# Cross attention of layer 2: keys projected first, key norms beside the queries, query norms in the score factors

## The chip, the cores and the metric

The kernel runs on one core of a Trainium2 chip. A core has five engines that run side by side and meet only through semaphores: TensorE (PE, matmul, writes the 8 banks of PSUM), VectorE (DVE), ScalarE (ACT), GpSimd (POOL) and SyncE (SP, which issues the loads here). The metric is the device time of one execution in microseconds (us), median of several runs.

## The reference, cut to what matters

x is 8 batches of 64 tokens of width 256 (512 tokens), the context 8 batches of 128 tokens (1024). Six residual stages follow each other: cross attention, attention and mixture of experts of layer 1, then the same three of layer 2. The change lies in the fourth, and touches the end of the third:

```python
def rms_norm(x, scale, eps=EPS):
    ms = jnp.mean(jnp.square(x), axis=-1, keepdims=True)
    return x * jax.lax.rsqrt(ms + eps) * scale
...
img_ctx = context[:, :N_IMG]
q = rms_norm(x @ q_w + q_b, nq_s).reshape(B, S, H, D)
k_img = rms_norm(img_ctx @ ki_w + ki_b, nki_s).reshape(B, -1, H, D)
v_img = (img_ctx @ vi_w + vi_b).reshape(B, -1, H, D)
out_img = sdpa(q, k_img, v_img)
return out @ o_w + o_b
```

The context has 128 tokens, fewer than N_IMG = 257, so all are image context and the text branch is over no tokens; H is 16, D 128. The norm of a query or key is over all 2048 features, that is over all 16 heads, so that no score is final before the last head is projected. x enters through a layernorm; the context doesn't, so the keys need nothing of the stages before.

## The kernel before, in words

Each matmul with weights is made of three (`mm3`, L153 to L155: hi x hi, hi x lo, lo x hi). ACT rounds a weight block to its hi part (`hi_part`, L206), POOL makes the lo part from it (`lo_part`, L215, raw minus hi). Blocks have a part a and a part b, two buffers each; `a_split`, `b_split` count finished parts, `a_used`, `b_used` parts that PE is done with. SP loads the next raw block once the split before it is made (`load_block`, L182 and L185).

The layer 2 cross attention (l1x) starts with the layernorm: DVE normalizes xn (L264), PE transposes it (L295) after `y_start` has put the output bias into banks 6 and 7 (L314), ACT and DVE write xt_hi and xt_lo (L303, L278). All of that waits for x, which the experts stage finishes with `ffn_add_half` (L1127), after its last `down` on PE.

Projections: for each head m, `proj_pe` makes 6 matmuls of 512 columns for the queries (part a, bank 4 + m%2), then 12 for the keys (part b, two banks). `proj_act` squares the queries out of PSUM (L1238) into sq and, one head late, the keys (`proj_keys`, L1228). POOL sums the squares of the queries (L1372), DVE those of the keys (`proj_acc`, L1245), with a wait for its own result behind it; DVE stores queries (qst, L1250, scaled by nqk) and keys (L1255). kst and qst keep all 16 heads.

Norms: when all sums are there, PE sums acc over the partitions (12 products with one column, L1323), DVE makes the variance (L1485), POOL the power -0.5 (L1382), DVE 12 diagonal tiles (L1487), PE spreads them over all partitions (3 banks, L1327), DVE places the key factors in rk (L1492), ACT copies the query factors to rq (L1418).

Attention: for each head ACT copies the keys to kn (L1446) and POOL multiplies the queries with rq into qn (L1389); PE makes the scores from both (`key_scores`, L1266), DVE multiplies them with rk (L1499) and goes through the softmax with ACT; PE transposes the weights (`turn_x`, L1275), mixes the context (`mix_ctx`, L1287), projects values (`values_x`) and output (`out_x`). PE's order is written out in `turn(m, u)`: turn_x(m-2), key_scores(m), values_x(m-3), mix_ctx(m-2), out_x(m-4). First and last turns are written out, the others are in a loop of the sequencer (`Fori`).

## Time and profile before

| | |
|---|---|
| median of 3 runs | 994.69 us (994.02 to 995.31) |
| the profiled execution | 994.79 us |
| its span in the trace | 993.0 us |
| PE busy | 880.0 us (89%) |
| DVE, ACT, POOL busy | 606.5, 427.2, 386.4 us |
| mean granted clock of PE | 0.864 |

A row of the timeline reads: start, duration, engine, line, operation, output<-inputs, how many were merged, and in brackets the idle time before with the one who ended it. PE's clock has two levels, 1.2 and 2.4 GHz; in a stretch 0.50 is all at the lower, 1.00 all at the higher. PEld is the load of weights and lies beside PE. Idle time of an engine that no one waits for costs nothing.

### The profile page before, as it was taken

To read this page: it belongs to the slowest core of one execution; us is meant where nothing else is said; L and a number is where in the kernel's file an instruction comes from. 1 tells how busy PE (TensorE), PEld (TensorE's weight loads), DVE (VectorE), ACT (ScalarE), POOL (GpSimd) and SP (SyncE) were. 2 spreads that over 40 slices of the span, in tenths; PEclk is the share of its full clock that TensorE was granted. 3 is DMA by queue.
4 is the path that set the end of the run, shared out by engine and by line. 5 is a ranking of instruction groups with operands and counts; after the bars stand their busy time and mean duration, and the time that the engine had idled before them with its cause. 6 is when DMAs were issued, how large, how long until landed. Compare 5 with 4: busy or idle time off the path is not lost.

```text
span 993.0 us, 17411 instructions
## 1 busy us (share of the span) xinstructions
PE 880.0 (89%) x6128; PEld 715.5 (72%) x6128; DVE 606.5 (61%) x931; ACT 427.2 (43%) x730; POOL 386.4 (39%) x414
## 2 busy tenths in 40 slices
PE   6489996899999599799769999978898699999997
PEld 5233334789889488588648999857887588888886
DVE  5989984466666457578556666445666344544543
ACT  2268882334433244255325555412222244555452
POOL 2168884133222134378423333111221144444442
PEclk8755555899999589699858999977999699999999
DMA  4059893022111023112100111100110123333331
GB/s 166 0 106 181 161 185 65 22 65 61 45 63 42 27 64 85 43 56 65 39 1 17 33 35 33 42 32 22 43 42 26 32 76 95 91 87 96 89 94 52
DMA packets 102530, 64.00 MB, mean 64 GB/s; under 512 B 71761, under 2 KB 90705, under 8 KB 102354
## 3 DMA queue, kind: packets, MB, share of 16 engines
q1 hardware_dynamic: 102482, 63.37, 24.6%
q8 instruction: 29, 0.48, 0.2%
q14 instruction: 19, 0.16, 0.1%
HBM read 46.05 MB, written 0.52 MB: 47 GB/s over the span
## 4 chain that ended last, share of the span: by engine, by line
PE 71%; DVE 13%; POOL 6%; issue 4%; ACT 3%; DMA 2%; SPq 0%; DVEq 0%; POOLq 0%; ACTq 0%
PE ps L153 18%; PE ps L155 16%; PE ps L154 16%; PE ps L1287 6%; POOL vf L609 4%; PE ps L1565 2%; PE ps L869 2%; PE ps L1566 2%; PE ps L1266 2%; DVE soft L1741 1%; POOL nb L616 1%; PE ps L880 1%; PE ps L314 1%; PE ps L1584 1%; DMA pti<-kres 1%
## 5 line engine op out<-in xcount | busy, mean ns | idle before, releaser
L215 POOL TENSOR_TENSOR wa_lo<-raw,wa_hi 128x512 fp32r<-128x512 f32 (+2 forms) x112 | 147.0, 1313 | 173.1 <-ACT wa_hi L206 170.3
L215 POOL TENSOR_TENSOR wb_lo<-raw,wb_hi 128x256 fp32r<-128x256 f32 (+1 forms) x112 | 92.0, 822 | 289.7 <-ACT wb_hi L206 289.7
L153 PE MATMUL ps<-xt_hi,wa_hi 128*128 128x512 f32 x352 | 147.8, 420 | 6.8 <-DVE xt_lo L278 4.4
L155 PE MATMUL ps<-xt_hi,wa_lo 128*128 128x512 f32 x352 | 144.4, 410 | 0.0
L154 PE MATMUL ps<-xt_lo,wa_hi 128*128 128x512 f32 x352 | 144.2, 410 | 0.0
L677 ACT ACTIVATE kres<-ps,nb,qs 128x1024 int16<-128x1024 f32 x64 | 77.0, 1203 | 28.3 <-POOL nb L616 26.1
L1111 DVE TENSOR_TENSOR hh<-sg,ps 128x512 f32<-128x512 f32 x56 | 38.5, 688 | 79.1 <-PE ps L155 74.4
L153 PEld LDWEIGHTS ps<-xt_hi,wa_hi 128*128 128x128 f32 x352 | 69.5, 198 | 22.7 <-issue 4.8
L798 DVE TENSOR_REDUCE nm<-ps 128x1 f32<-128x1024 f32 x64 | 78.1, 1223 | 10.3 <-PE ps L556 8.9
L1113 DVE TENSOR_TENSOR h_lo<-hh,h_hi 128x512 fp32r<-128x512 f32 x56 | 58.3, 1042 | 40.6 <-ACT h_hi L1103 40.6
L206 ACT ACTIVATE wa_hi<-raw 128x512 fp32r<-128x512 f32 (+2 forms) x112 | 66.7, 595 | 35.7 <-PE ps L155 30.5
L155 PEld LDWEIGHTS ps<-xt_hi,wa_lo 128*128 128x128 f32 x352 | 69.5, 198 | 16.6
L154 PEld LDWEIGHTS ps<-xt_lo,wa_hi 128*128 128x128 f32 x352 | 69.8, 198 | 13.0
L153 PE MATMUL ps<-wb_hi,h_hi 128*128 128x256 f32 (+1 forms) x240 | 68.1, 289 | 4.3 <-DVE h_lo L1113 4.3
L609 POOL CAST vf<-pti 128x1024 bf16<-128x1024 int16 x64 | 66.2, 1036 | 7.0 <-DMA pti<-kres 3.5
L556 PE MATMUL ps<-qkt 48*128 48x512 bf16 x128 | 64.8, 618 | 4.5 <-ACT kres L677 1.5
L1097 ACT ACTIVATE sg<-ps 128x512 f32<-128x512 f32 x56 | 33.5, 598 | 79.7 <-PE ps L155 79.7
L154 PE MATMUL ps<-wb_lo,h_hi 128*128 128x256 f32 (+1 forms) x240 | 66.8, 283 | 0.0
L155 PE MATMUL ps<-wb_hi,h_lo 128*128 128x256 f32 (+1 forms) x240 | 66.8, 283 | 0.0
L1287 PEld LDWEIGHTS ps<-ptx,ctx 128*128 128x128 f32 x512 | 62.8, 201 | 1.9 <-issue 0.6
L153 PE MATMUL ps<-wb_hi,ot_hi 128*128 128x256 f32 x192 | 60.1, 313 | 4.1 <-DVE ot_lo L1717 2.5
L1287 PE MATMUL ps<-ptx,ctx 128*128 128x64 f32 x512 | 62.3, 283 | 0.2 <-ACT ptx L1428 0.2
(254 smaller groups left out, 2016.3 us busy)
## 6 DMA issues: line engine op xcount, KB each, us to landing
raw<-w_l1f SPq DMA_DIRECT2D x44, 256.0 KB, 2.7
raw<-w_l0a SPq DMA_DIRECT2D x16, 384.0 KB, 3.2
raw<-w_l1f SPq DMA_DIRECT2D x44, 128.0 KB, 2.0
raw<-w_l1p SPq DMA_DIRECT2D x32, 128.0 KB, 2.1
raw<-w_l1x SPq DMA_DIRECT2D x32, 128.0 KB, 2.1
raw<-w_l1a SPq DMA_DIRECT2D x16, 256.0 KB, 3.0
raw<-w_l0f SPq DMA_DIRECT2D x12, 256.0 KB, 2.7
raw<-w_l0a SPq DMA_DIRECT2D x16, 128.0 KB, 2.3
```

Source lines behind the costliest of these rows:

```text
L153: nc.tensor.matmul(o, a[0], b[0], start=start, stop=False, **kw)
L154: nc.tensor.matmul(o, a[0], b[1], start=False, stop=False, **kw)
L155: return nc.tensor.matmul(o, a[1], b[0], start=False, stop=stop, **kw)
L206: nc.scalar.activation(dst[:, u, 0:cols.stop - cols.start], raw[:, u, cols], ACT.Copy).then_inc(done, 1)
L215: nc.gpsimd.tensor_tensor(lo[:, u, 0:w], raw[:, u, cols], hi[:, u, 0:w].bitcast(F32), ALU.subtract).then_inc(done, 1)
L556: last = nc.tensor.matmul(slot(n)[:, j * 512:(j + 1) * 512], qkt[64 * a:64 * a + 48, u, t * P:(t + 1) * P], qkt[64 * a:64 * a + 48, u, NTO ...
L609: nc.gpsimd.tensor_copy(pt[:, r, :], pti[:, r, :]).then_inc(x0["pt"], 1)
L677: nc.scalar.activation(ei[:, n % RING, :], slot(n), ACT.Exp, bias=nb[:, n % 3:n % 3 + 1], scale=qs[:, col:col + 1], accum_out=sums[:, u, k ...
L798: nc.vector.tensor_reduce(nm[:, n % 3:n % 3 + 1], slot(n), AX.X, ALU.max, negate=True).then_inc(x0["nm"], 1)
L1111: nc.vector.tensor_tensor(hh[:, u, :], sg[:, u, :], ps[:, 2 * u + 1, :], ALU.mult).then_inc(ff["h"], 1)
L1113: nc.vector.tensor_tensor(h_lo[:, u, :], hh[:, u, :], h_hi[:, u, :].bitcast(F32), ALU.subtract).then_inc(ff["hlo"], 1)
L1287: last = nc.tensor.matmul(ps[:, 3 + c, b * T:(b + 1) * T], ctx[:, b, c * P:(c + 1) * P], ptx[:, g, T * p:T * (p + 1)], start=True, stop=True)
```

## The change

All 16 key projections come first, directly behind the last down projection of the experts stage; y_start and the layernorm's transposes stand on PE behind key 2, the 16 query projections behind key 15. Weights are loaded in that order, as 32 parts of 128 x 256, alternating between the a and the b buffers (`load_projections`). ACT and POOL make three of these parts still in the experts stage or right behind it. Queries have three banks (3, 0, 1), keys two pairs (2, 3 and 4, 5). The squares of the queries are summed in two accumulators: POOL takes heads 1, 5, 7, 9, 11 and 13, DVE the other ten. The key norms are made between the queries: column sums behind query 3, variance and power around 4, diagonal at 6, spreading behind query 9, placing at 11. The query norms are no longer multiplied into the queries: 16 small products put the squares' sums straight into the layout of the scores (behind key_scores(0)), and DVE multiplies the result into rk. kn, qn, rq and the clearing of acc go. All loops of this stage are written out.

```diff
+        def load_projections(sp):
+            for j in range(2 * H):
+                n, w, off = L1P[0] + j // 2, L1P[2], 0 if j >= H else L1P[2]
+                split, loaded_ = (a_split, a_loaded) if j % 2 == 0 else (b_split, b_loaded)
+                sp.wait_ge(split, n - 1)
+                sp.dma_start(raw[:, n % 2, w * (j % 2):w * (j % 2 + 1)], w_l1p[j % H, :, off:off + w]).then_inc(loaded_[n % 2], 16)
...
-        acc = sb("acc", [P, 1536], ctx=mc)
+        acc = sb("acc", [P, 2048], ctx=mc)
...
             lo_parts(pool, L0F, L1P, 2)
+            head_part(lo_part, pool, 1)
...
             peeled(act, CH0, chunk)
+            for j in range(1, AHEAD):
+                head_part(hi_part, act, j)
...
+        AHEAD, QUERIES, LN_AT, MS_AT, ONES_AT = 4, H, 3, 3, 9
...
+        def proj_key(pe, m):
+            bank = 2 + 2 * (m % 2)
+            pe.wait_ge(split_of(m), block_of(m) + 1)
+            if m == 0:
+                pe.wait_ge(ff["h"], CH0)
+            elif m == 1:
+                pe.wait_ge(ff["ev"], CH0 - 1)
+            else:
                 pe.wait_ge(l1["kst"], m - 1)
...
+        def proj_query(pe, m):
+            j = QUERIES + m
+            pe.wait_ge(split_of(j), block_of(j) + 1)
+            if m == 0:
+                pe.wait_ge(l1["kst"], H - 1)
+            if m >= 3:
+                pe.wait_ge(l1["qst"], m - 2)
+            for c in range(C2):
+                last = mm3(ps[:, QBANKS[m % 3], :], weights_of(j, c), (xt_hi[:, c, :], xt_lo[:, c, :]), c == 0, c == 1)
+            last.then_inc(used_of(j), 1)
...
+        def key_squares(act, m):
             act.wait_ge(l1["kst"], m + 1)
+            if m >= 1:
                 act.wait_ge(l1["acck"], m)
...
+        def query_squares(act, m):
+            j = QUERIES + m
+            act.wait_ge(used_of(j), block_of(j) + 1)
+            if m == 1:
+                act.wait_ge(l1["acck"], H)
+            elif m >= 2:
+                act.wait_ge(*summed(m - 2))
...
         def key_scores(pe, m, u):
-            pe.wait_ge(l1["qn"], m + 1)
-            pe.wait_ge(l1["kn"], m + 1)
+            if m < 2:
+                pe.wait_ge(l1["qst"], H - 2 + m)
...
-                last = nc.tensor.matmul(..., qn[:, u, b * T:(b + 1) * T], kn[:, u, b * S:(b + 1) * S], start=True, stop=True)
+                last = nc.tensor.matmul(..., qst[:, m, b * T:(b + 1) * T], kst[:, m, b * S:(b + 1) * S], start=True, stop=True)
...
         def l1x_pe(pe):
+            for m in range(H):
+                if m == LN_AT:
+                    pe.wait_ge(x_ready, 6)
+                    y_start(R_OB)
+                    ln_pe(pe, 3)
+                proj_key(pe, m)
             pe.wait_ge(ln_lo, 8)
+            for m in range(H):
+                proj_query(pe, m)
+                if m == MS_AT:
+                    pe.wait_ge(l1["acck"], H)
...
+                if m == ONES_AT:
+                    pe.wait_ge(l1["diag"], 1)
...
+            def query_means():
+                pe.wait_ge(*summed(H - 1))
+                pe.wait_ge(*summed(H - 3))
...
+            for m in range(H + 4):
                 turn(m, m % 2)
...
         def l1x_pool(pool):
             ln_pool(pool, 3)
-            lo_part(pool, "b", 0, NP, L1P)
-            nc.gpsimd.memset(acc[:], 0.0).then_inc(l1["acc0"], 1)
...
+            for m in range(H):
+                head_part(lo_part, pool, QUERIES + m + AHEAD)
+                if by_pool(m):
+                    query_acc(pool, m)
+                if m == MS_AT + 1:
+                    root(slice(0, NKT), 1)
+            root(slice(NKT, NKT + NT), 3)
...
         def l1x_act(act):
             load_table(act, ACT.Exp)
+            for m in range(H):
+                if m == LN_AT:
+                    ln_act(act, 3)
+                head_part(hi_part, act, m + AHEAD)
+                key_squares(act, m)
+            for m in range(H):
+                head_part(hi_part, act, QUERIES + m + AHEAD)
+                query_squares(act, m)
...
         def l1x_dve(dve):
+            ln_dve_norm(dve, 3)
+            for m in range(H):
+                if m == LN_AT:
+                    ln_dve_split(dve, 3)
+                key_store(dve, m)
+                if m >= 1:
+                    key_acc(dve, m - 1)
+            key_acc(dve, H - 1)
...
+            for m in range(H):
+                if m == H - 1:
+                    query_acc(dve, m)
+                query_store(dve, m)
+                if not by_pool(m) and m < H - 1:
+                    query_acc(dve, m)
...
+            variance(slice(NKT, NKT + NT), ps[:, 2, NKT:NKT + NT], 4)
+            dve.wait_ge(l1["var"], 4)
             dve.wait_ge(l1["placed"], 1)
+            nc.vector.tensor_tensor(rk, rk, rms[:, NKT:NKT + NT].unsqueeze(2).broadcast_to([P, NT, S]), ALU.mult).then_inc(l1["placed"], 1)
+            dve.wait_ge(l1["placed"], 2)
```

## Rows read from the trace of the kernel before

**Rows 1.** The page: the chain that ended last, by engine.

```profile
PE 71%; DVE 13%; POOL 6%; issue 4%; ACT 3%; DMA 2%; SPq 0%; DVEq 0%; POOLq 0%; ACTq 0%
```

**Rows 2.** Stretches: from:to length, PE, PEld, DVE, ACT, POOL busy, PEclk, DMA share, GB/s.

```profile
404.60:416.40 11.80, 8.39 (x24) 5.14 (x24) 8.28 (x24) 2.70 (x7) 1.87 (x3) 0.51 0.00 0
416.40:421.70 5.30, 5.28 (x12) 4.13 (x13) 0.81 (x1) 1.15 (x3) 4.69 (x7) 0.50 0.24 76
421.70:488.00 66.30, 63.58 (x277) 51.80 (x275) 52.77 (x46) 36.78 (x60) 50.08 (x45) 1.00 0.20 60
488.00:506.60 18.60, 10.04 (x30) 6.74 (x31) 4.53 (x5) 2.68 (x4) 3.74 (x3) 0.63 0.00 0
512.00:540.00 28.00, 26.16 (x173) 23.66 (x174) 19.45 (x29) 11.34 (x18) 5.09 (x5) 0.72 0.05 15
```

**Rows 3.** Timeline at the seam from the experts stage to the cross attention.

```profile
404.62 0.39 PE L153 MATMUL ps<-wb_hi,h_hi 128*128 128x256 f32 x1 [2.23 <-DVE h_lo L1113]
...
409.33 3.78 PE L314 MATMUL ps<-row,ones 1*128 1x512 f32 x4 [2.00 <-DVE x L1127]
...
411.46 0.74 DVE L264 TENSOR_SCALAR xn<-x,mv,rstd 128x256 f32<-128x256 f32 x2 [0.27 <-POOL rstd L288]
...
416.42 0.80 PE L153 MATMUL ps<-xt_hi,wa_hi 128*128 128x512 f32 x1 [1.41 <-DVE xt_lo L278]
...
420.20 0.81 DVE L1250 TENSOR_SCALAR qst<-ps,vec,nqk 128x512 f32<-128x512 f32 x1 [3.84 <-ACT soft L1238]
```

**Rows 4.** Instructions on kst, qst and acc: ns min/median/max, first and last start.

```profile
L1255 DVE TENSOR_SCALAR kst<-ps,vec x16: 1282/1284/1285, 423.4 to 486.2; 128x1024 f32 x14, 128x1024 f32<-128x1024 f32 x2
L1228 ACT ACTIVATE soft<-kst x16: 1051/1062/1067, 425.4 to 487.5; 128x1024 f32 x14, 128x1024 f32<-128x1024 f32 x2
...
L1250 DVE TENSOR_SCALAR qst<-ps,vec,nqk x16: 808/810/815, 420.2 to 483.6; 128x512 f32 x14, 128x512 f32<-128x512 f32 x2
...
L1372 POOL TENSOR_TENSOR acc<-acc,soft x16: 1276/1296/1303, 420.1 to 483.5; 128x512 f32<-128x512 f32 x16
L1245 DVE TENSOR_TENSOR acc<-acc,soft x16: 1224/1394/1475, 426.5 to 488.6; 128x1024 f32<-128x1024 f32 x16
```

**Rows 5.** Timeline inside the projection loop, one turn of its end.

```profile
477.92 1.28 DVE L1255 TENSOR_SCALAR kst<-ps,vec 128x1024 f32 x1 [0.27 <-DVE acc L1245]
...
480.38 0.40 ACT L206 ACTIVATE wa_hi<-raw 128x256 fp32r<-128x256 f32 x1
480.50 1.23 DVE L1245 TENSOR_TENSOR acc<-acc,soft 128x1024 f32<-128x1024 f32 x1 [0.25 <-ACT soft L1228]
...
480.85 1.48 POOL L215 TENSOR_TENSOR wa_lo<-raw,wa_hi 128x256 fp32r<-128x256 f32 x1 [0.23 <-ACT wa_hi L206]
...
482.00 1.28 DVE L1255 TENSOR_SCALAR kst<-ps,vec 128x1024 f32 x1 [0.27 <-DVE acc L1245]
...
482.29 0.74 POOL L215 TENSOR_TENSOR wb_lo<-raw,wb_hi 128x256 fp32r<-128x256 f32 x1
```

**Rows 6.** Timeline from the last projection to the first scores.

```profile
489.90 4.93 PE L1323 MATMUL ps<-ones,acc 128*128 128x1 f32 x24 [4.62 <-issue]
...
495.19 2.27 POOL L1382 TENSOR_TENSOR rms<-rms,neghalf 128x12 f32<-128x12 f32 x1 [10.38 <-DVE rms L1485]
497.50 1.76 DVE L1487 TENSOR_TENSOR acc<-ident,rms 128x1536 f32<-128x1536 f32 x1 [2.39 <-POOL rms L1382]
...
503.13 1.39 DVE L1492 COPY xn<-ps 64x512 f32<-64x512 f32 x2 [3.87 <-PE ps L1327]
...
508.09 0.69 DVE L1499 TENSOR_TENSOR soft<-ps,xn 128x512 f32<-128x512 f32 x1 [3.57 <-PE ps L1266]
```

**Rows 7.** Timeline of the attention: the first weights' transposes, two later heads' scores.

```profile
512.61 1.12 PE L1275 MATMUL ps<-ident,soft 128*128 128x128 f32 x4 [2.83 <-DVE soft L1512]
...
599.28 0.69 DVE L1499 TENSOR_TENSOR soft<-ps,xn 128x512 f32<-128x512 f32 x1 [0.71 <-PE ps L1266]
...
607.38 0.69 DVE L1499 TENSOR_TENSOR soft<-ps,xn 128x512 f32<-128x512 f32 x1 [0.71 <-PE ps L1266]
```

More of the change, by code:

```diff
@@ L1225, in proj_keys, with row_of, by_pool, summed @@
+        def row_of(buf, m):
+            return buf[:, m:m + 1, :].rearrange("p a n -> p (a n)")
+        def by_pool(m):
+            return m % 2 == 1 and m not in (3, H - 1)
+        def summed(m):
+            return (l1["accp"] if by_pool(m) else l1["accq"]), sum(by_pool(k) == by_pool(m) for k in range(m + 1))
+        QBANKS = (3, 0, 1)
+        def query_square(m):
+            return sq[:, 0:512] if m % 2 else sq[:, 1024:1536]
+        def key_squares(act, m):
             act.wait_ge(l1["kst"], m + 1)
-            if exists(m, m - 1):
+            if m >= 1:
@@ new lines, in query_acc @@
+        def query_acc(eng, m):
+            own = acc[:, 1536:2048] if by_pool(m) else acc[:, 1024:1536]
+            done, count = summed(m)
+            eng.wait_ge(l1["sqq"], m + 1)
+            if m < 2:
+                last = (nc.gpsimd if by_pool(m) else nc.vector).tensor_copy(own, query_square(m))
+            else:
+                last = (nc.gpsimd if by_pool(m) else nc.vector).tensor_tensor(own, own, query_square(m), ALU.add)
+            last.then_inc(done, 1)
+            eng.wait_ge(done, count)
@@ L1265, in key_scores @@
                 p, g = place(b)
-                last = nc.tensor.matmul(ps[T * p:T * (p + 1), u, g * S:(g + 1) * S], qn[:, u, b * T:(b + 1) * T], kn[:, u, b * S:(b + 1) * S], start=True, stop=True)
+                last = nc.tensor.matmul(ps[T * p:T * (p + 1), u, g * S:(g + 1) * S], qst[:, m, b * T:(b + 1) * T], kst[:, m, b * S:(b + 1) * S], start=True, stop=True)
             last.then_inc(l1["s"], 1)
@@ L1391, in turn @@
-            def turn(i, u):
-                m = 2 * i + u
-                if within(m):
-                    head(m, u)
-                split_x(lo_part, pool, i, u)
-            for i in range(2):
-                for u in range(2):
-                    turn(i, u)
-            with pool.Fori(2, H // 2) as i:
-                for u in range(2):
-                    turn(i, u)
-            for u in range(3):
-                turn(H // 2, u)
+            for j in range(2, AHEAD):
+                head_part(lo_part, pool, j)
@@ L1530, in turn @@
                     mixed(m - 2)
[L1532 to L1537 removed]
+            for m in range(H + 3):
                 turn(m, m % 2)
```

204 lines of the change are left out of this document (71 added, 133 removed).

## The prediction

> **What bounds the kernel now.** I read the page's chain that ended last first: 71% of the span is TensorE (PE) [rows 1]. The change touches only the cross attention of layer 2, so I cut the span into stretches there [rows 2], then read the order of time at the two seams [rows 3, 6], the durations of one instruction [rows 4] and one turn of the projection loop [rows 5].
>
> Four pieces show up. (a) 404.6 to 416.4 us: PE works 8.4 of 11.8 us at half clock (PEclk 0.51). It waits 2.23 us for h_lo, then 2.00 us for x, then for the layernorm; the first projection matmul starts at 416.42 and the first store of VectorE (DVE), qst, at 420.20 [rows 2, 3]. (b) 421.7 to about 485 us: projections, PE without a hole. One head takes 4.08 us (two kst rows, 477.92 and 482.00) [rows 5]: 18 matmuls at 0.227 us. DVE has 0.81 (qst) + 1.28 (kst) + 1.39 (acc) + a 0.27 wait for its own sum = 3.75 us [rows 4, 5], so PE ends last, but only by 0.33 us a head. (c) 485.3 to 508.1 us: a serial tail. PE idles 4.62 us, makes 24 small products, PE waits for POOL's power (2.27), DVE's diagonal (1.76), six wide products, DVE's placing (1.39), then rq and qn. The first scores leave PE's bank at 508.09 [rows 6]. (d) the attention loop, 8.10 us a head (599.28, 607.38), in which DVE waits 0.71 us for PE at every head [rows 7]: PE alone sets it.
>
> **Attention loop, kn and qn copies, unrolling: nothing.** The change drops 16 ACT copies and 16 POOL products and writes the loops out. In (d) both engines only serve PE, whose instructions stay the same; the cover is PE's own work, and would it go, the cost would be the copies again. Loop turns cost PE nothing in (b): 63.6 us busy of 66.3 us, and the missing 2.7 us are the hole that starts at 485.3 [rows 2, 6]. Bounds: 0 to 1 us gained; I take 0.
>
> **Start.** PE no longer waits for x: key 0 follows the last down projection, whose end is 409.33 - 2.00 = about 407.3 [rows 3]. Twelve matmuls at the lower level take 12 x 0.44 = 5.3 us (12 instructions fill the 5.3 us from 416.4) [rows 2]; so key 0 is there by 412.6 at worst, by 411.3 if the clock returns underway. DVE has the layernorm's first half until 411.46 + 0.74 = 412.2 [rows 3] and then stores key 0. DVE's projection work starts 8 us earlier than before (420.20). POOL's roots for the layernorm stand behind one more lo part (0.74 us [rows 5]), which its 7 us of idleness there hide. ACT's table load and SP's later loads have more slack than they need: the next use of a slot is four parts away.
>
> **Key part: DVE, not PE, ends last.** PE needs 12 x 0.227 = 2.72 us a key. DVE needs 1.283 (store) + acc + 0.27 + 0.06 between. The trace has acc from 1.224 to 1.475 us [rows 4]; 1.23 is the row in which it started ahead of POOL's lo part (480.50) and the lo part, 0.73 alone, took 1.48 [rows 5]. In the changed order acc k may start 0.27 + 1.28 + 0.06 = 1.61 us after acc k-1 ends. The next lo part needs the square (1.06), a hi part (0.40) and three handovers of about 0.07, 1.67 us. So acc starts first, narrowly, and I take 1.25: 2.86 us a key, 0.14 above PE.
> Sum from 412.2: stores 16 x 1.283 = 20.5; sums 16 x 1.25 = 20.0 (the first is a copy, priced the same); own waits 16 x 0.27 = 4.3; gaps 1.0; keys 1 and 2 not ready 0.9; layernorm split at key 3: DVE waits for the third square and two ACT copies (1.4) and does two 0.69 us pieces, 2.8; the last square, which no store covers, 1.1. That is 50.6, and the keys end at 462.8. y_start and the transposes (at most 7.1 us at the lower level [rows 3]) stand on PE between keys 2 and 3 and end before ACT asks for them.
>
> **The seam between keys and queries: a new hole on PE.** Query 0 needs the store of key 14, at about 456. Queries 0, 1 and 2 have banks and take 3 x 1.36 = 4.1 us, till 460.3. Query 3 reuses the bank of query 0, so it waits for the store of query 0, which stands in DVE's order behind store 15 and the last three sums: 462.8 + 0.8 + 0.1 = 463.9 or so. Hole: 3.6 us. Before, PE's clock fell at the end of a 2.23 us hole (404.62: the next stretch has 0.51) and needed the 5.3 us from 416.42 to return [rows 2, 3]. I expect it to fall here too.
> The Trainium skill, "TensorE: Matmul & The Clock Gate", section "HAM oscillation — how this bites in real kernels", says that waits between bursts of matmuls put the array back to its half clock each time; this trace agrees. By that rule the 3.9 us below are paid; without it the sum is 981.4.
>
> **Query part.** PE 1.36 us a query; DVE 16 x (0.81 + 0.05) = 13.8; ten sums of half the keys' width, 10 x (0.70 + 0.27) = 9.7 (0.61 to 0.74 by halving rows 4, plus POOL's blocking); variance, a diagonal of 8 instead of 12 tiles (1.76 x 2/3 = 1.17) and the placing (1.39), 3.0 with gaps; DVE waiting for POOL, where root and sums follow each other, 1.0. Together 27.5, about 1.7 us a query against PE's 1.36. POOL has 16 lo parts of 0.74 and six sums of 1.29 [rows 4, 5], 20 us plus the root (below 2.27), and stays a little below DVE. The last store (0.9) lies beside the norm, so the last sum ends at T = 462.8 + 26.6 = 489.4 with PE at full clock. At half clock queries 3 to 5 take 12 x 0.44/2 = 2.6 us each and the 16 small products for the key norms 3.3 instead of 1.6 us (24 took 4.93 [rows 6]); of these 5.4 extra us DVE's own backlog, which those queries would have met, covers a part. Bounds 2.8 to 5.0, I take 3.9: T = 493.3.
>
> **New tail.** Key norms are done beside the queries. After T: 32 small instructions (4.93/24 = 0.205 at half clock, so 0.10 at full: 3.3, less with their halved width; I take 2.8), variance 0.2, POOL's power of 4 columns (between a third of 2.27 and all of it; I take 1.0), DVE's product into rk (0.7 by the 128x512 row at 508.09), handovers 0.6: 5.3 us [rows 6]. Scores of heads 0 and 1 are on PE in that time. First scores are read at 498.6 instead of 508.09: 9.5 us earlier. Behind it the attention starts as before: PE then idles until the first weights come, 4.5 us later (512.61 - 508.09) [rows 6, 7], and its clock is half either way (0.72 over 512 to 540 [rows 2]).
>
> **Sum.** The profiled execution took 994.79 us (span 993.0), 0.1 above the median of 994.69. 994.79 - 9.5 = 985.3. Bounds: key sums -0.5 to +3.6; query sums and POOL's blocking -1 to +3; seam -3.9 to +1.1; tail -1 to +1.5; key 1 late at half clock up to +2.5; phase of the clock in the attention's start +-2. They don't all fall together.
>
> **Rivals.**
> 1. The clock doesn't fall at the seam (for: 60 us of dense work before; against: the 2.23 us hole): 985.3 - 3.9 = 981.4. Chance 9%.
> 2. The attention starts at full clock. Half clock held for 28 x (1 - 0.72)/0.5 = 15.7 us there [rows 2]; PE would win up to 7.8, of which DVE's chain keeps some 3: 980.3. Against it: the same 4.5 us hole precedes it. 7%.
> 3. POOL gets to SBUF first. The margin of acc over the lo part is 0.06 us a key. If the lo part starts first at each key, acc takes 1.23 + up to 0.73 = 1.95 us, DVE 3.56 a key, 16 x 0.7 = 11.2 more: 996.5, slower than before. It decides when the lo part starts before acc in more than four fifths of the keys; at half of them the time is 991. For: the lo part of 1.48 us and acc's spread to 1.475 show that one waits for the other [rows 4, 5]. Against: no acc above 1.475. 12%, a third of it above 996.
> The Trainium skill, "SBUF — State Buffer", section "Who interferes with whom", says that VectorE and GpSimd hold their common port pair for a whole instruction while the other stands still; the 1.48 us lo part agrees.
> 4. DVE's slower pace leaves holes on PE, and half clock holds through all queries: 13 x 2.6 + 3.3 + ones 3.4 = 40.5 from 463.9, 504.4; square and sum 1.8, tail 8.5 at that clock: 514.7, 6.6 later than before, 1001.4. It decides when more than about eight queries run at half. Against: holes of 0.3 us in 1.7. 5%.
>
> **Chances.** Forecast (982 to 989) 63%, rivals 9, 7, 12 and 5%, anything else 4%. Range 979 to 992: it takes in rivals 1 and 2 and the milder half of 3. A measurement of this kernel tells 0.2% (2 us) from no change; faster than 992.7: 86%, within: 5%, slower: 9%.
>
> **What would show it.** kst stores from about 412, 2.8 to 2.9 us apart, acc at 1.22 to 1.3 us; a PE hole of 3 to 4 us after the third query and PEclk 0.5 behind it; last query sum near 493; first scores 5 us on, near 499; then 8.10 us a head. It is wrong if kst stores stand 3.2 us or more apart, if queries take over 2 us each to the end, or if the first head turns differ from the old ones by more than 2 us.

## The result, and the profile after

| kernel | median us | lowest to highest, runs | profiled execution, its span | granted clock |
|---|---|---|---|---|
| before | 994.64 | 994.02 to 995.31, 4 | 994.79, 993.0 | 0.864 |
| after | 973.04 | 970.75 to 973.97, 4 | 970.75, 969.0 | 0.885 |

The changed kernel is faster: the ratio of the two is 0.9779, with a 95% interval of 0.9761 to 0.9798. It saves 21.6 us by the medians, where 9.5 were forecast. The direction was right and the time lies below the range.

To find where the time went, cut both spans at work that both kernels have. The first variance row of a layernorm (`vareps`) marks where a stage has its x; the first read of the scores marks where the attention begins. DVE's timeline of the kernel before has the first two of these rows, and [rows 6] the first scores (508.09); the second fence is the kernel after.

```profile
337.75 0.17 DVE L258 TENSOR_SCALAR vareps<-mv 128x2 f32<-128x2 f32 x1
...
408.33 0.17 DVE L258 TENSOR_SCALAR vareps<-mv 128x2 f32<-128x2 f32 x1
```

```profile
334.77 0.17 DVE L266 TENSOR_SCALAR vareps<-mv 128x2 f32<-128x2 f32 x1
...
403.88 0.17 DVE L266 TENSOR_SCALAR vareps<-mv 128x2 f32<-128x2 f32 x1
...
486.75 0.69 DVE L1549 TENSOR_TENSOR soft<-ps,xn 128x512 f32<-128x512 f32 x1
```

With the two later variance rows (before 652.17 and 780.35, after 629.49 and 756.74) this gives, in us:

| stretch | before | after | gained | touched by the change |
|---|---|---|---|---|
| start to the experts of layer 1 | 337.75 | 334.77 | 2.98 | no |
| experts of layer 1 | 70.58 | 69.11 | 1.47 | loads at its end |
| first variance to first scores | 99.76 | 82.87 | 16.89 | yes |
| first scores to the next stage's variance | 144.08 | 142.74 | 1.34 | loops written out, kn and qn gone |
| self attention of layer 2 | 128.18 | 127.25 | 0.93 | no |
| experts of layer 2 to the end | 212.65 | 212.26 | 0.39 | no |

The third row, "the projection stretch" below, was forecast at 9.5 us gained and brought 16.9. Two things that were not forecast stand beside it: the experts stage, and stages whose code is the same. A second trace of the same kernel (label after_again below) helps to sort these out.

The kernel after at the seam from the experts to the keys, the timeline:

```profile
390.05 24.07 SPq L203 DMA_DIRECT2D raw<-w_l1p  x11
...
393.27 0.42 ACT L214 ACTIVATE wa_hi<-raw 128x256 fp32r<-128x256 f32 x1 [0.54 <-PE ps L155]
...
400.17 0.39 PE L153 MATMUL ps<-wb_hi,h_hi 128*128 128x256 f32 x1 [1.39 <-DVE h_lo L1118]
...
401.70 0.40 PE L153 MATMUL ps<-ct_hi,wa_hi 128*128 128x512 f32 x1
...
408.07 2.46 DVE L1297 TENSOR_SCALAR kst<-ps,vec 128x1024 f32<-128x1024 f32 x2
...
409.49 0.47 PE L153 MATMUL ps<-ct_hi,wa_hi 128*128 128x512 f32 x1 [2.14 <-POOL wa_lo L223]
```

and of the kernel before, the rows on ACT and SP that answer to the first two:

```profile
396.68 0.34 SPq L182 DMA_DIRECT2D raw<-w_l1p  x1
...
398.86 0.42 ACT L206 ACTIVATE wa_hi<-raw 128x256 fp32r<-128x256 f32 x1 [3.07 <-DMA raw<-w_l1p]
```

Before, SP issued the first projection weights at 396.68, and ACT stood 3.07 us for them with the experts' h_hi queued behind: that made the 2.23 us hole of [rows 3]. Now the load is issued 3 us ahead of its use (390.05 against 393.27), ACT no longer waits for it, and the hole is 1.39 us. Key 0 follows the last down projection without a gap (401.70). Stretches of the kernel after (columns as in [rows 2]):

```profile
401.70:407.00 5.30, 5.30 (x26) 4.33 (x24) 4.63 (x16) 2.32 (x4) 1.52 (x3) 1.00 0.09 25
407.00:415.10 8.10, 5.96 (x25) 3.65 (x24) 6.57 (x7) 2.87 (x5) 4.08 (x6) 1.00 0.24 73
415.10:457.00 41.90, 40.09 (x178) 32.85 (x177) 35.66 (x31) 22.06 (x34) 22.65 (x15) 1.00 0.15 43
457.00:483.00 26.00, 23.33 (x114) 17.56 (x113) 22.25 (x28) 13.21 (x25) 20.16 (x20) 1.00 0.25 71
...
486.90:503.60 16.70, 12.13 (x68) 11.10 (x70) 11.44 (x19) 4.19 (x7) 0.06 (x1) 0.50 0.00 1
```

In this trace PE's clock stays at its upper level (2.4 GHz) from the experts to the first scores. The half-clock stretch at the start of the stage in [rows 2] (0.51, 0.50) is gone, and the one forecast between keys and queries never comes. Inside the keys, the timeline of the kernel after (it answers to [rows 5]): two rows from a place where DVE is late, then one turn of the steady state.

```profile
425.19 1.22 DVE L1305 TENSOR_TENSOR acc<-acc,soft 128x1024 f32<-128x1024 f32 x1
426.44 1.28 DVE L1297 TENSOR_SCALAR kst<-ps,vec 128x1024 f32<-128x1024 f32 x1
...
431.86 1.28 DVE L1297 TENSOR_SCALAR kst<-ps,vec 128x1024 f32<-128x1024 f32 x1 [0.30 <-PE ps L155]
...
433.06 1.22 DVE L1305 TENSOR_TENSOR acc<-acc,soft 128x1024 f32<-128x1024 f32 x1
433.10 1.78 POOL L223 TENSOR_TENSOR wa_lo<-raw,wa_hi 128x256 fp32r<-128x256 f32 x1 [0.94 <-ACT wa_hi L214]
...
434.58 1.28 DVE L1297 TENSOR_SCALAR kst<-ps,vec 128x1024 f32<-128x1024 f32 x1 [0.30 <-PE ps L155]
```

The stores stand 2.72 us apart and wait 0.30 us each for PE: here PE sets the pace, not DVE. What DVE itself needs shows in the first two rows, where the key is ready: the sum ends at 426.41 and the next store starts 0.03 us later, though the program waits there for the sum's own result. In the kernel before, the same wait took 0.27 to 0.29 us in each of the 14 turns that are in the sequencer's loop, and 0.03 us (426.48 + 1.48 = 427.96 to 427.99) in the one turn with a sum and a next store that is written out:

```profile
426.48 1.48 DVE L1245 TENSOR_TENSOR acc<-acc,soft 128x1024 f32<-128x1024 f32 x1
427.99 1.28 DVE L1255 TENSOR_SCALAR kst<-ps,vec 128x1024 f32<-128x1024 f32 x1
...
432.47 1.28 DVE L1255 TENSOR_SCALAR kst<-ps,vec 128x1024 f32 x1 [0.29 <-DVE acc L1245]
```

So the 0.27 us went with the loop. No run writes out the projection loops of the kernel before alone, so these rows are all that ties it to the loop. The end of the keys and the first queries, DVE's timeline, and under it all waits of PE from 415 us to the tail:

```profile
454.58 1.23 DVE L1305 TENSOR_TENSOR acc<-acc,soft 128x1024 f32<-128x1024 f32 x1 [1.26 <-ACT soft L1282]
455.84 0.81 DVE L1310 TENSOR_SCALAR qst<-ps,vec,nqk 128x512 f32<-128x512 f32 x1
```

```profile
456.80 0.47 PE L153 MATMUL ps<-xt_hi,wb_hi 128*128 128x512 f32 x1 [1.81 <-DVE qst L1310]
...
469.67 1.98 PE L1394 MATMUL ps<-acc,ones 128*128 128x512 f32 x4 [1.08 <-DVE acc L1532]
...
479.21 0.47 PE L153 MATMUL ps<-xt_hi,wb_hi 128*128 128x512 f32 x1 [0.52 <-DVE qst L1310]
...
483.24 1.20 PE L1405 MATMUL ps<-ones,acc 128*64 128x1 f32 x29 [1.31 <-DVE acc L1320]
```

The keys end at 455.81 (454.58 + 1.23) and the last query sum at 483.09 (482.40 + 0.69). From there the tail is short (it answers to [rows 6]), DVE's and POOL's timeline:

```profile
482.40 0.69 DVE L1320 TENSOR_TENSOR acc<-acc,soft 128x512 f32<-128x512 f32 x1 [0.33 <-ACT soft L1292]
...
486.02 0.69 DVE L1543 TENSOR_TENSOR xn<-xn,rms 128x512 f32<-128x512 f32 x1 [1.20 <-POOL rms L1445]
```

```profile
484.96 1.02 POOL L1445 TENSOR_TENSOR rms<-rms,neghalf 128x4 f32<-128x4 f32 x1 [3.44 <-DVE rms L1520]
```

### The profile page after: what moved, and what is told of

The parts are those of the page before. It is cut to its first block, busy times and chain, and to the rows that moved or that the text cites. A ratio compares the mean times of both kernels' runs of the same rounds, so it can differ in the third digit from the quotient of the medians.

```text
span 969.0 us, 16903 instructions
## 1 busy us (share of the span) xinstructions
PE 861.4 (89%) x6150; PEld 702.2 (72%) x6150; DVE 612.8 (63%) x943; ACT 410.2 (42%) x713; POOL 352.9 (36%) x388
## 4 chain that ended last, share of the span: by engine, by line
PE 69%; DVE 16%; POOL 5%; issue 4%; ACT 3%; DMA 2%; DVEq 0%; SPq 0%; POOLq 0%; ACTq 0%
PE ps L153 16%; PE ps L155 15%; PE ps L154 15%; PE ps L1354 6%; PE ps L561 4%; PE ps L1610 2%; DVE x L1124 2%; POOL vf L614 2%; PE ps L1611 2%; PE ps L874 2%; PE ps L1333 1%; PE ps L570 1%; DVE soft L1786 1%; PE ps L885 1%; PE ps L1629 1%
## 5 line engine op out<-in xcount | busy, mean ns | idle before, releaser
L223 POOL TENSOR_TENSOR wb_lo<-raw,wb_hi 128x256 fp32r<-128x256 f32 (+1 forms) x112 | 94.9, 848 | 299.6 <-ACT wb_hi L214 299.6
L153 PE MATMUL ps<-xt_hi,wa_hi 128*128 128x512 f32 x336 | 141.0, 420 | 5.4 <-DVE xt_lo L286 3.0
L154 PE MATMUL ps<-xt_lo,wa_hi 128*128 128x512 f32 x336 | 136.8, 407 | 0.0
L155 PE MATMUL ps<-xt_hi,wa_lo 128*128 128x512 f32 x336 | 136.8, 407 | 0.0
L153 PEld LDWEIGHTS ps<-xt_hi,wa_hi 128*128 128x128 f32 x336 | 66.2, 197 | 20.6 <-issue 4.3
L155 PEld LDWEIGHTS ps<-xt_hi,wa_lo 128*128 128x128 f32 x336 | 65.9, 196 | 15.7
L154 PEld LDWEIGHTS ps<-xt_lo,wa_hi 128*128 128x128 f32 x336 | 66.4, 198 | 12.2 <-issue 0.2
```

What stands on the lines that cost most here:

```text
L153: nc.tensor.matmul(o, a[0], b[0], start=start, stop=False, **kw)
L154: nc.tensor.matmul(o, a[0], b[1], start=False, stop=False, **kw)
L155: return nc.tensor.matmul(o, a[1], b[0], start=False, stop=stop, **kw)
L223: nc.gpsimd.tensor_tensor(lo[:, u, 0:w], raw[:, u, cols], hi[:, u, 0:w].bitcast(F32), ALU.subtract).then_inc(done, 1)
```

## The experiments

Theory A was formed on the trace after: the extra gain is (1) weights loaded earlier at the experts' end, and (2) no fall of PE's clock, because the hole between keys and queries is 1.8 us and not 3.6. The rivals are the recorded steps: that the hole costs its 3.9 us all the same when it is as long as forecast, that DVE sets the query part, that key norms beside the queries or the late x are worth nothing, that written-out loops matter. All medians stand beside runs of the kernel before on the same chip: 993.14, 991.95, 992.10 and 991.98 us in the four groups of runs. These medians hide something: the kernel before has two groups of times there. 20 of its 54 runs took 985.4 to 989.0 us, 31 took over 991.9, and only three lie between, while the ten runs of the kernel after lie within 970.8 to 974.9. The three traces of kernels with the old order are all of slower runs (994.8, 992.0 and 995.0 us), so the stretches below are those of the slower group; against the faster one the change gains some 14 us. No trace shows where that group is faster, and this stays open. The ratios against these groups have intervals of up to 1% with it. What follows was run in the order of the questions, not of time. "Projection stretch" is as in the table above.

**The changed kernel again**, unchanged, beside the last experiments:

> The changed kernel once more, unaltered, on the same chip as the next runs. Theory A (the 3 us that the first trace gained before the changed stage, in the attention of layer 1, are chance of PE's clock): that stage takes 164.5 to 167.2 us as in the other runs, whichever kernel; the stretch from the variance of this stage's layernorm to the first scores repeats within 0.5 us of 82.9. Theory B (the change moved the early stages too): about 164.6 again and again.

It took 973.58 us, ratio 0.9828 (0.9790 to 0.9865), 18.5 us less than before on that chip. Its projection stretch was 83.18 and its experts stage 68.45 us: 16.6 + 2.1 = 18.7 us gained in the two places that the change touches (18.4 in the first trace). That the medians on this chip give nearly the same is luck, since the one of the kernel before falls between its two groups of times. The self attention of layer 1, whose code is the same in all kernels here, shows what the rest is: 167.20 us in the trace before, 164.61 in the one after, and in the first step of the better version (below) 164.81 in one run and 166.95 in the next. The self attention of layer 2 took 127.25 us in the first trace of the kernel after and 132.01 in the second. So, against the trace before, some 18.5 us belong to the two places that the change touches, and the rest of the 21.6 us (24.0 in the two profiled executions) lies in stages whose code is the same or whose pace PE sets as before, and is within their spread.

**Late load**: SP waits with the first key's part a for one split more, as the old loader did.

```diff
                 sp.wait_ge(split, n - 1)
+                if j == 0:
+                    sp.wait_ge(b_split, n - 1)
                 sp.dma_start(raw[:, n % 2, w * (j % 2):w * (j % 2 + 1)], w_l1p[j % H, :, off:off + w]).then_inc(loaded_[n % 2], 16)
```

> The changed kernel, in which the first load of key weights again waits for both lo parts of the block before, as load_block does in the kernel before. Theory A (the new load order, a thing the forecast gave no price, shortened the experts stage's end): ACT waits again for that load for about 3 us in the last chunk, the hole on PE before the last down projection grows from 1.39 to about 2.2 us or more, the second layernorm's first variance of this stage moves 0.8 to 1.5 us later against the start of the experts stage, and if the clock falls there the end comes 2 to 5 us later. Theory B (the stage's 1.47 us are chance of the clock): within 0.5 us.

976.02 us, ratio 0.9832 (0.9788 to 0.9875). The timeline shows the old picture again, and the stretch behind the hole is at half clock:

```profile
397.51 0.42 ACT L216 ACTIVATE wa_hi<-raw 128x256 fp32r<-128x256 f32 x1 [3.11 <-DMA raw<-w_l1p]
...
403.27 0.43 PE L153 MATMUL ps<-wb_hi,h_hi 128*128 128x256 f32 x1 [2.23 <-DVE h_lo L1120]
```

```profile
403.00:407.00 4.00, 3.73 (x15) 3.52 (x16) 3.68 (x12) 0.94 (x3) 0.81 (x1) 0.57 0.10 33
407.00:415.00 8.00, 7.34 (x33) 5.76 (x32) 6.91 (x15) 3.47 (x6) 4.91 (x7) 1.00 0.18 49
```

The experts stage took 70.33 us, 1.2 to 1.9 more than in the two traces of the kernel after. The projection stretch did not change (82.89): with key 0 right behind the downs, PE was back at its upper level by 407. So the load order is shown to be worth 1 to 2 us. All sixteen traces agree: the experts stage took 70.2 to 70.6 us in the four with the old load order and 68.4 to 69.2 in the twelve with the new one.

**Early load, in the kernel before**: the same wait taken from the old loader.

```diff
-                if isinstance(n, int):
+                if isinstance(n, int) and stage is not L1P:
                     sp.wait_ge(b_split, n - 1)
```

> The kernel before with one wait less: the loads of the first two key and query weight blocks no longer wait for the lo part of the b weights two blocks back before their first part is fetched. Theory A (the load order alone ended the 3.07 us wait of ACT and the half clock at the first seam): the hole before the last down projection falls from 2.23 to about 1.4 us, 1 to 2 us are gained there, and PE may keep its clock through the down projection, though not through the layernorm behind it. In all -1 to -3 us against the kernel before. Theory B: nothing, within 0.5 us.

990.74 us, ratio 0.9994 (0.9968 to 1.0019): the time alone says nothing. The trace does: a hole of 1.39 us before the last down, experts stage 69.10 instead of 70.58 us, projection stretch 98.88 instead of 99.76. That is 2.4 us in the stages concerned, which the spread of the whole time hides.

**x first**: the new order, but PE builds the bias and transposes x ahead of key 0.

```diff
-        AHEAD, QUERIES, LN_AT, MS_AT, ONES_AT = 4, H, 3, 3, 9
+        AHEAD, QUERIES, LN_AT, MS_AT, ONES_AT = 4, H, 0, 3, 9
```

> The changed kernel with y_start and the transposes of the layernorm ahead of key 0, so that PE waits for x as before; all else stays. PE then stands idle 2.0 us, works 2 us on the bias, waits for xn, transposes, some 9 us in all, before key 0. Theory A (DVE's order sets the pace, so that the early start brings 8 us as by the forecast): +6 to +9 us, and half clock in keys 0 and 1. Theory B (the early keys bring little because DVE and PE stand in each other's way later): under +3 us.

975.42 us, ratio 0.9822 (0.9782 to 0.9863); projection stretch 86.77, 3.9 us more than after. PE's timeline and stretches:

```profile
407.97 3.12 PE L322 MATMUL ps<-row,ones 1*128 1x512 f32 x4 [3.02 <-DVE x L1132]
```

```profile
403.00:407.00 4.00, 1.70 (x12) 1.49 (x12) 3.68 (x12) 2.00 (x4) 0.79 (x1) 1.00 0.20 56
407.00:415.00 8.00, 7.03 (x18) 4.31 (x19) 5.25 (x14) 1.20 (x2) 3.25 (x5) 0.60 0.10 33
```

The 3.9 us lie between the two theories. The wait for x is back (3.02 us), and the clock behind it is down. Key 0 starts 7.9 us later against the first variance, but half of that returns: in the kernel after PE does the same bias and transposes a little later and has the 2.14 us hole among the keys as well. The 8 us by which DVE started earlier in the forecast were thus never 8 us of gain.

**Key norms not beside the queries**: PE's 16 small products and its ones products, POOL's root, DVE's diagonal and placing all stand behind the last query.

```diff
                 proj_query(pe, m)
-                if m == MS_AT:
-                    pe.wait_ge(l1["acck"], H)
...
+            pe.wait_ge(l1["acck"], H)
+            for t in range(NKT):
...
+            pe.wait_ge(l1["diag"], 1)
```

> The changed kernel with all steps of the key norms (column sums, variance, power, diagonal, spreading, placing) behind query 15 instead of between the queries. Serial they take 1.84 + 0.2 + 1.7 + 1.2 to 2.2 + 2.0 + 1.4 = about 9 us by the rows; the queries get shorter, since DVE has 3 to 4 us less and PE 3.8 us less between them. Theory A (hiding them is worth the serial time less that relief): +4 to +6 us, more by 1 to 3 if PE's clock falls in the new tail earlier. Theory B (DVE's waits in the query part grow with them hidden, so hiding brings nearly nothing): under +2 us.

979.91 us, ratio 0.9875 (0.9832 to 0.9918); projection stretch 87.17, 4.3 us more than after. PE's timeline, and DVE's:

```profile
485.38 3.78 PE L1392 MATMUL ps<-acc,ones 128*128 128x512 f32 x4 [5.21 <-DVE acc L1527]
```

```profile
484.10 1.23 DVE L1527 TENSOR_TENSOR acc<-ident,rms 128x1024 f32<-128x1024 f32 x1 [1.82 <-POOL rms L1443]
...
493.86 0.69 DVE L1543 TENSOR_TENSOR soft<-ps,xn 128x512 f32<-128x512 f32 x1
```

Its last query sum ends at 481.35 and its scores are read at 493.86: a tail of 12.5 us. The kernel before has 18.3 (489.79 to 508.09) and the kernel after 3.66. So what this kernel shares with the one after (4 wide products instead of 6, a power and a product over 4 columns, no rq and qn) goes with a tail 5.8 us shorter, and moving the key norms takes another 8.8 us out of it, of which the query part pays 4.5 back. Part of the 8.8 is the clock: it fell behind the 5.21 us hole, and the four wide products took 3.78 us there against 1.98 at the upper level between the queries.

**Written-out loops, in the kernel before**: its attention loops written out and the 16 kn copies left out.

```diff
-            pe.wait_ge(l1["kn"], m + 1)
...
-            for m in range(4):
-                turn(m, m % 2)
-            with pe.Fori(2, H // 2) as i:
-                for u in range(2):
-                    turn(2 * i + u, u)
-            for m in range(H, H + 4):
+            for m in range(H + 4):
                 turn(m, m % 2)
```

> The kernel before with the attention loops of this stage written out and the copies of keys to kn left out (scores read kst at once); the product into qn stays. The forecast prices both at 0 to 1 us gained, since PE alone sets the 8.10 us a head. Theory A: 0 to -1 us. Theory B (the 1.34 us that the attention lost in the trace of the changed kernel come from these two edits): -1 to -2 us, at the first heads behind the start.

990.15 us, ratio 0.9992 (0.9963 to 1.0020); projection stretch 99.86 (before 99.76), attention 143.87 (144.08). The attention's loops and copies cost nothing, as forecast. The projection loops stayed in this run, so it says nothing of them.

**A longer hole between keys and queries, twice.** DVE gets extra work ahead of the store of query 0: two statistics of x (0.75 us), or these and a maximum over x (1.97 us).

```diff
             dve.wait_ge(l1["nqk"], 1)
+            for k in range(2):
+                nc.vector.bn_stats(stats[:, k % NT, :], x[:, k % NT, :])
```

```diff
             dve.wait_ge(l1["nqk"], 1)
+            nc.vector.tensor_reduce(mx[:, 0:NT], x[:], AX.X, ALU.max)
+            for k in range(2):
+                nc.vector.bn_stats(stats[:, k, :], x[:, k, :])
```

> The changed kernel with two extra DVE instructions (statistics of x, 0.75 us together) ahead of the store of query 0; their result is used by nothing. It widens the hole on PE ahead of query 3 from 1.81 to about 2.5 us. Theory A (the forecast's price was right and the hole was only too short): the hole comes near the 2.23 us one of the kernel before, behind which PEclk was 0.5, so the clock may fall: 0.75 plus up to 3.9, about +4. Theory B (the clock does not fall behind a single hole of this size after 45 us of dense work): +0.3 to +0.8 us on the changed kernel.

> The changed kernel with 1.97 us of extra DVE work (a reduction and two statistics of x, results unused) ahead of the store of query 0. The hole on PE ahead of query 3 becomes about 3.8 us, the size that the forecast had. Theory A: PEclk falls to 0.5 behind it and the step costs 1.97 plus 2.8 to 5.0, so +5 to +7 us. Theory B: the clock stays, +1.5 to +2.0 us.

The shorter: 975.15 us, ratio 0.9829 (0.9788 to 0.9870). The longer: 978.09 us, ratio 0.9852 (0.9812 to 0.9891). PE's timeline and stretches of the shorter:

```profile
458.22 0.47 PE L153 MATMUL ps<-xt_hi,wb_hi 128*128 128x512 f32 x1 [2.46 <-DVE qst L1310]
```

```profile
457.00:465.00 8.00, 6.78 (x38) 5.88 (x39) 6.04 (x11) 3.81 (x9) 3.98 (x6) 1.00 0.23 68
```

and of the longer:

```profile
463.15 0.47 PE L153 MATMUL ps<-xt_hi,wb_hi 128*128 128x512 f32 x1 [3.58 <-DVE qst L1310]
```

```profile
463.00:471.00 8.00, 7.85 (x29) 6.98 (x30) 3.94 (x7) 1.68 (x3) 0.73 (x2) 0.59 0.14 43
```

A hole of 2.46 us left the clock up, and the projection stretch was 83.55, 0.7 more for 0.75 us of extra work. A hole of 3.58 us, the size that was forecast, brought it down for about 7 us, and the stretch was 87.63: 4.8 more than after (4.6 with the mean of its two traces), of which 2.0 are the extra work and some 2.7 the clock.

**Small sums**: eight of the ten query sums on DVE add 8 columns instead of 512, which takes 4.7 us off DVE in the query part (its sums after the first take 2.63 us together instead of 7.30).

```diff
-                last = (nc.gpsimd if by_pool(m) else nc.vector).tensor_tensor(own, own, query_square(m), ALU.add)
+                w = 512 if by_pool(m) or m == H - 1 else 8
+                last = (nc.gpsimd if by_pool(m) else nc.vector).tensor_tensor(own[:, 0:w], own[:, 0:w], query_square(m)[:, 0:w], ALU.add)
```

> The changed kernel in which DVE's sums of the query squares of heads 2, 3, 4, 6, 8, 10, 12 and 14 are only 8 columns wide instead of 512, so the query norms are not the reference's. About 0.6 us are taken from each of 8 sums, 5 us in all. Theory A (DVE sets the query part, as by the forecast): the stretch from the last key sum to the last query sum, 27.3 us, falls by 3.5 to 5. Theory B (PE with the norm's products between, and the handovers, set it): by under 2 us.

973.24 us, ratio 0.9821 (0.9772 to 0.9870). From the end of the keys to the last query sum it is 25.25 us instead of 27.3: 2.0 us, not 4.7, at the edge of theory B. It leaves most of the squares out, so its query norms are wrong; the order of its instructions is the same. PE's holes say which:

```profile
459.42 0.47 PE L153 MATMUL ps<-xt_hi,wb_hi 128*128 128x512 f32 x1 [1.81 <-DVE qst L1310]
480.55 0.47 PE L153 MATMUL ps<-xt_hi,wb_hi 128*128 128x512 f32 x1 [0.26 <-DVE qst L1310]
483.83 1.20 PE L1406 MATMUL ps<-ones,acc 128*64 128x1 f32 x29 [0.59 <-DVE acc L1321]
```

The hole at the diagonal is gone (1.08 us), the one at the end of the queries is 0.26 shorter, the last wait 0.72 shorter: 2.06 together. DVE sets the query part at these three places only; elsewhere PE does.

**The three parts undone together**: late load, x first and serial key norms in one kernel (the three diffs above).

> The changed kernel with three of its parts undone at once: late first load, layernorm ahead of key 0, key norms behind query 15. One by one they moved the stage's traces by 1.2 us (experts stage's end), 3.8 and 4.2 us (stretch to the first scores, 82.9 to 83.2). Theory A (the parts add up): experts stage 70.3 us, stretch 91.0 us; what then is left to the 99.8 us of the kernel before, near 9 us, is the order keys first and the query norms in the factors. Theory B (they overlap in DVE's or PE's slack, or share one fall of the clock): stretch under 89 us.

984.15 us, ratio 0.9935 (0.9907 to 0.9963). Experts stage 70.45 and projection stretch 92.42 us. The single runs add up to 82.87 + 3.9 + 4.3 = 91.1, so they are additive within 1.4 us. The remaining 7.3 us to the 99.76 of before are the keys' own order, the written-out projection loops and the query norms in the factors, which I did not separate by a run; the tail's 5.8 us (18.3 - 12.5) would be most of it.

**A better version, in two steps.** First, DVE stores query 0 ahead of the last key sum, ACT squares query 0 ahead of the last key square, and POOL makes the third lo part ahead of the layernorm's roots:

```diff
+            head_part(lo_part, pool, 2)
             ln_pool(pool, 3)
...
+                if m == H - 1:
+                    head_part(hi_part, act, QUERIES + AHEAD)
+                    query_squares(act, 0)
                 key_squares(act, m)
...
-            key_acc(dve, H - 1)
             dve.wait_ge(l1["nqk"], 1)
+            query_store(dve, 0)
+            key_acc(dve, H - 1)
```

> The changed kernel with two changes of order. POOL makes the lo part for key 2 ahead of the roots of the layernorm (PE waited 2.14 us for it), and ACT squares query 0 ahead of the last keys, so that DVE stores query 0 in the 1.26 us in which it waits for that square; query 3 then finds its bank free. Theory A (the keys wait for DVE and PE alike, and the hole of 1.81 us stands on the path through DVE): key part 0.5 to 1.5 us shorter, query part 1 to 2 us shorter, -1.5 to -3.5 us against the changed kernel. Theory B (DVE's own load sets both parts): under 0.5 us.

> The version with query 0 squared ahead of the last keys, again, beside the changed kernel itself. Its stretch to the first scores was 80.87 against 82.87 us. Theory A (a gain on the path stays): -2 us against the changed kernel in the median. Theory B (given back by the attention behind it, where its trace showed 143.7 instead of 142.7 us): under 1 us.

973.18 and 972.00 us, ratios 0.9820 (0.9788 to 0.9852) and 0.9814 (0.9776 to 0.9853). The projection stretch was 80.87 and 80.83, 2.0 to 2.4 less than after; on the second chip the median is 1.6 us below the kernel after, too little to tell by the times alone. PE has no hole before query 3 any more. The hole before key 2 stayed at 2.14 us with another releaser:

```profile
409.49 0.47 PE L153 MATMUL ps<-ct_hi,wa_hi 128*128 128x512 f32 x1 [2.14 <-DVE kst L1297]
```

The early lo part thus bought nothing; key 2 needs the bank of key 0, whose store stands in DVE's order behind the layernorm. So the second step puts DVE's normalizing behind the first two keys, and PE's transposes two keys later:

```diff
-        AHEAD, QUERIES, LN_AT, MS_AT, ONES_AT = 4, H, 3, 3, 9
+        AHEAD, QUERIES, LN_AT, MS_AT, ONES_AT = 4, H, 5, 3, 9
...
-            ln_dve_norm(dve, 3)
             for m in range(H):
+                if m == 2:
+                    ln_dve_norm(dve, 3)
```

> The version with query 0 first, and the layernorm moved further back: DVE stores keys 0 and 1 before it normalizes x, PE transposes behind key 4. PE's 2.1 us hole ahead of key 2 should go, and with it DVE's wait of 1.4 us. The key part is then 16 x 2.72 plus 2.7 us of bias and transposes: the stretch to the first scores 2 to 2.6 us shorter, 78.3 to 78.9 us. Rival: the layernorm's halves then wait for each other in the middle of the keys, where DVE has 0.3 us to spare, and under 1 us is gained.

> The version with the layernorm behind key 4, once more. Theory A (that its attention took 139.7 instead of 142.7 to 144.1 us, because PE's clock came back at 492 us and not behind the first values, is chance of one run): attention 142.7 to 144.1 us this time, and times spread over 965 to 973 us. Theory B (the clock's return there hangs on the order of work ahead and repeats): 139.5 to 140 us again and times of 965 to 969 us.

967.30 and 966.95 us, ratios 0.9773 (0.9734 to 0.9811) and 0.9771 (0.9717 to 0.9824); the projection stretch was 78.76 both times, 4.1 less than after. PE's holes before key 2 and before query 3 are both gone; between the experts' last one (0.97 us) and the tail only that at the diagonal (1.09) is over 0.9 us. The kernel after took 973.58 us on the chip of the first of these runs: this version is 6.3 us faster than it. Its attention took 139.72 us in one trace and 143.44 in the other. The stretches of the first, then of the second, show why:

```profile
483.00:492.00 9.00, 3.62 (x25) 2.52 (x22) 6.98 (x11) 1.74 (x3) 0.34 (x1) 0.50 0.00 0
492.00:496.00 4.00, 4.00 (x35) 4.00 (x36) 3.19 (x6) 0.68 (x2) 0.00 (x0) 0.94 0.02 4
```

```profile
492.00:496.00 4.00, 3.79 (x19) 3.63 (x18) 3.33 (x6) 0.75 (x2) 0.00 (x0) 0.50 0.00 0
496.00:503.00 7.00, 7.00 (x39) 6.24 (x39) 3.47 (x5) 1.95 (x4) 0.73 (x1) 0.50 0.01 2
```

The same program came back to the upper clock at 492 in one run and after 503 in the other, and 3.7 us hang on it.

## Why the prediction was wrong, point by point

**Start: right in kind, unforeseen in one queue.** Key 0 did follow the last down without waiting for x. The forecast looked at the later loads only and put the stage in front at nothing, and that step failed: the new loader also asks for the first key weights earlier than the old one did. The gain lies at the end of the preceding stage (1 to 2 us, late load and early load), a place in which nothing had been counted. DVE's first key store came 4.19 us after the first variance (408.07 - 403.88) against 3.9 forecast.

**Key part: ended 2.5 us earlier than forecast.** It took 51.93 us from the first variance, against 54.5. The step that failed is "DVE, not PE, ends last", at 2.86 us a key. Where DVE does not wait for PE it takes 2.45 us (423.99 to 426.44): 1.20 from store to sum instead of 1.28 + 0.06, 1.22 for the sum instead of 1.25, and 0.03 behind it instead of the own wait of 0.27. The last of these differences is the largest, on a term of 16 x 0.27 = 4.3 us in the forecast's sum; it was read from looped turns [rows 5] and carried over to code without a loop. So PE's 2.72 us set the pace, 32.7 us over the 12 keys from store 3 to store 15 instead of 34.3, which is 1.6 us; another 0.56 is the first sum, a copy of 0.69 us and not 1.25. Had the 0.27 stayed, DVE would need 2.69 us, by this estimate still below PE's 2.72, but with 0.03 instead of 0.27 us a key to make up what the layernorm's split and one blocked sum cost it. The square did start only when the sum before it ended, as assumed.

**Rival 3, POOL first: happened at one key.** The margin of 0.06 us a key was called right: acc starts at 433.06 and the lo part at 433.10, so acc takes its own 1.22 and the lo part 1.78 instead of the 0.74 of [rows 5]. Once, at 422.18, the lo part started first (422.14) and the sum took 1.77 us. The Trainium skill, "SBUF — State Buffer", section "Who interferes with whom", has the later of the two wait out the whole instruction of the other; these rows agree to within 0.2 us, and so does the diagonal: 2.20 us beside POOL's work in the kernel after, 1.23 us alone in the serial kernel.

**Seam between keys and queries: where the failed pace cost most.** The hole was forecast at 3.6 us because DVE, at 2.86 us a key, was to fall behind PE and come to the store of query 0 only at 462.8. With PE setting the keys' pace DVE has no backlog there, only the last square and sum. The hole was 1.81 us, and the clock stayed up. Rival 1 (9%) is what happened. Its price was right in kind: with a hole of 3.58 us the clock fell and cost some 2.7 us, just under the 2.8 to 5.0 in the text. The query part took 27.3 us from the keys' end instead of 30.5, 3.2 of the 7.4 us missed.

**Query part at full clock: right number, wrong reason.** 26.6 us was forecast with DVE as the one that ends last, 27.3 measured. The ten own waits of 0.27, 2.7 us of that sum, are 0.03 to 0.05 us each here as well (the sum at 458.90 ends at 459.58, the next store starts at 459.63). And taking 4.7 us off DVE gave only 2.0. PE was busy for 23.33 of 26 us there, and its own list is 13 queries, the 16 small and 4 wide products and the first scores; DVE delays it by 1.08 + 0.52 + 1.31 us.

**Tail: 3.66 us, forecast 5.3.** The 32 small products were put at 2.8 us, from 24 in 4.93 at half clock [rows 6]. The first 29 took 1.20 us: 0.04 us each, with weights of 64 columns. The forecast had already counted the upper clock (0.10 each, 3.3 us); what it had too large is the product with 64 columns. The 16 products for the key norms, with 128 columns and at the upper clock too, took 1.84 us, 0.115 each. POOL's power was 1.02 (1.0 forecast), DVE's product 0.69 (0.7).

**Attention, copies, loops: right.** Nothing gained beyond the spread of 142.7 to 144.1 us that 15 of the 16 traces here have. PE waits 5.71 us before the first transposes and its clock is half from 486.9 to 503.6, so rival 2 did not come true in the kernel after (its own terms give 985.3 - 7.8 + 3 = 980.5, not 980.3). Rival 4 did not either.

**Sum.** 2.54 (keys) + 3.22 (seam and query part) + 1.64 (tail) = 7.4 us missed in the projection stretch, to which come 1.5 in the experts stage. 9.5 + 7.4 + 1.5 = 18.4 of the 21.6 us; the other 3.2 (5.6 in the two profiled executions) are stages with unchanged code or, in the attention, an unchanged pace. The range had an end for nearly each of these terms, but let only one or two fall at a time. The first two fell together because they hang on one assumption, that DVE and not PE sets the keys' pace; the third is a size of its own, that of the small products. Those 3.2 us are spread and no merit of the change; all four runs of the kernel before in the result belong to its slower group of times, so 21.6 us is the upper end of what the change saves. The forecast's "0.2% (2 us) from no change" is too fine for a kernel whose times spread over 10 us.

## What to carry to other kernels

Before pricing a hole, work out which engine sets the pace ahead of it, with and without the small terms: here a forecast margin of 0.14 us a turn decided between a hole of 1.8 and one of 3.6 us, and with it between clocks. When a change writes a loop out, read the small waits from a turn that was already written out, not from the loop. Terms that follow from one assumption miss together, so the range has to add them. When a change rewrites a loader, compare the time at which each load is issued with the one before, for the stage in front as well; and when an order is changed, look at what stands ahead of the first store that frees a bank, as the last version did.

## What the runs showed of the hardware

- **The length of a hole does not decide alone whether PE's clock falls.** It stayed up behind holes of 1.39, 1.81, 2.14 to 2.19 (eight traces) and 2.46 us, and fell behind 2.23 to 2.25 (four traces, the kernel before and the late load among them), 3.02 and 3.58 us. Between 2.23 (fell) and 2.46 (stayed) the order is the wrong way round, so something besides the length decides; what it is stays open. The same hole can go either way: behind the 1.3 us one at the start of the tail the clock stayed up until the scores in the kernel after, and in the second trace of the same kernel it had fallen by 484:

```profile
482.80 1.38 PE L1405 MATMUL ps<-ones,acc 128*64 128x1 f32 x29 [1.30 <-DVE acc L1320]
```

```profile
484.00:485.00 1.00, 1.00 (x14) 1.00 (x14) 0.16 (x1) 0.00 (x0) 0.16 (x1) 0.50 0.00 0
```

The Trainium skill, "TensorE: Matmul & The Clock Gate", section "HAM oscillation — how this bites in real kernels", has the clock fall at each wait between bursts, and the waits that it describes are of 3 to 5 us. The holes of 3.02 and 3.58 us agree; the forecast took that rule for a hole that turned out at 1.81 us, and the fall at 2.23 us lies outside it.
- **The return is chance of several us.** In two runs of the same program it came at 492 and after 503, for 3.7 us of time.
- **Stages with the same code differ by 2 to 3 us from run to run, once by nearly 5**, in either kernel (164.5 or 167.2 us for the layer 1 attention, 127.25 or 132.01 for that of layer 2), so a change worth 2 us shows in the stretch of the trace that it touches (early load) where the time can't tell it.
- **Products with one column are cheap:** 0.04 us each with weights of 64 columns and 0.115 with 128 at the upper clock, 0.205 with 128 at half clock.
- **A wait for an engine's own result costs next to nothing in written-out code:** DVE's took 0.03 to 0.05 us there and 0.27 to 0.29 us in the turns of a loop.
